# Four stretches of 64-column products in place of six, in each round of a perceiver layer's attention

## What is computed

```python
x = x + _L0_xattn_ref(_layernorm(x), ctx_1024, ctx_1024, mask, gamma, beta)   # softmax(q.k) @ v, layernorm
x = x + _L0_attn_ref(_layernorm(x), W_qkv, W_out)                             # one head of 512
x = x + _L0_ffn_ref(_layernorm(x), router_w, expert_w1, expert_w2)            # top 2 of 8 experts
```

## Time and profile before

| what | us |
|---|---|
| median of 3 runs | 757.66 (757.39 to 758.61) |
| profiled execution | 757.7 |
| span of the profiled execution | 756.0 |
| TensorE busy | 735.9 (97% of the span) |
| VectorE busy | 439.4 (58%) |
| ScalarE busy | 310.5 (41%) |
| Pool engine busy | 155.7 (21%) |

### The profile page before, as it was taken

The page is one execution under the profiler, slowest core; times in us unless marked ns, Lnnn a source line. Parts: engine busy times, 40 slices in busy tenths (PEclk is TensorE's granted clock), DMA queues, the critical chain, the costliest instruction groups (busy, mean ns, idle before and its releaser), DMA issues.

```text
span 756.0 us, 12377 instructions
## 1 busy us (share of the span) xinstructions
PE 735.9 (97%) x4786; PEld 557.9 (74%) x4786; DVE 439.4 (58%) x1003; ACT 310.5 (41%) x520; POOL 155.7 (21%) x162
## 2 busy tenths in 40 slices
PE   7999999999999999999999999999999999999996
PEld 5443454545546454478999999999999899888885
DVE  5324456676767673868865454555555665565631
ACT  2122212121212131345456455555565665656631
POOL 2132030505041301123401301310211311120201
PEclk9999999999999999999999999999999999999998
DMA  9999999999999999930635635745665756674602
GB/s 319 406 422 416 395 400 418 402 418 402 418 399 420 400 416 405 374 116 31 205 125 197 189 113 197 199 148 216 163 222 167 217 190 206 238 203 175 177 2 28
DMA packets 36477, 199.40 MB, mean 264 GB/s; under 512 B 4716, under 2 KB 5372, under 8 KB 15680
## 3 DMA queue, kind: packets, MB, share of 16 engines
q1 hardware_dynamic: 29912, 186.74, 64.3%
q0 software_dynamic: 4704, 9.14, 6.6%
q10 hardware_dynamic: 1800, 2.70, 1.1%
HBM read 188.19 MB, written 10.37 MB: 263 GB/s over the span
## 4 chain that ended last, share of the span: by engine, by line
PE 84%; DMA 7%; DVE 4%; SPq 2%; issue 1%; ACT 1%; POOL 0%; POOLq 0%
PE ps L850 11%; PE ps L809 9%; PE ps L1074 8%; PE ps L1076 8%; PE ps L1075 8%; PE ps L1096 4%; PE ps L1098 4%; PE ps L1097 4%; PE ps L1105 4%; PE ps L1106 4%; PE ps L1107 4%; PE ps L865 3%; DMA arena<-in_w_qkv 3%; DMA arena<-in_ctx 3%; PE ps L777 2%; DVE low_a L1519 2%
## 5 line engine op out<-in xcount | busy, mean ns | idle before, releaser
L481 POOL TENSOR_TENSOR small<-small 128x1 f32<-128x1 f32 x64 | 24.8, 388 | 551.2 <-DVE yb_space L1688 196.2
L1289 ACT ACTIVATE hid<-ps 128x288 f32<-128x288 f32 (+5 forms) x128 | 50.6, 396 | 145.1 <-PE ps L1076 140.9
L1076 PE MATMUL ps<-xT,low_a 128*128 128x288 f32 (+5 forms) x384 | 110.1, 287 | 0.0
L1657 DVE TENSOR_TENSOR h_ring<-hid,h_ring 128x288 fp32r<-128x288 f32 (+5 forms) x128 | 55.6, 435 | 85.2 <-ACT h_ring L1294 85.1
L850 PE MATMUL ps<-arena 128*64 128x512 f32 (+1 forms) x416 | 95.4, 599 | 1.7 <-DMA arena<-in_ctx 0.9
L1519 DVE TENSOR_TENSOR low_a<-w_raw_a,high_b 128x2048 fp32r<-128x2048 f32 x32 | 73.2, 2292 | 37.8 <-ACT high_b L1214 37.8
L809 PE MATMUL ps<-arena 128*64 128x512 f32 x384 | 85.7, 596 | 0.8 <-DMA arena<-in_ctx_turned 0.6
L1154 ACT COPY arena<-ps 128x512 f32<-128x512 f32 (+2 forms) x90 | 42.0, 526 | 100.3 <-PE ps L784 62.5
L1074 PE MATMUL ps<-xT,high_b 128*128 128x288 f32 (+5 forms) x256 | 74.9, 292 | 0.0
L1075 PE MATMUL ps<-xT,high_b 128*128 128x288 f32 (+5 forms) x256 | 73.4, 287 | 0.0
L1076 PEld LDWEIGHTS ps<-xT,low_a 128*128 128x128 f32 x384 | 72.4, 189 | 0.0
(11 more groups left out here) (217 smaller groups left out, 1639.3 us busy)
## 6 DMA issues: line engine op xcount, KB each, us to landing
arena<-in_ctx_turned SPq DMA_DIRECT2D x48, 1024.0 KB, 22.7
arena<-in_ctx SPq DMA_DIRECT2D x48, 1024.0 KB, 19.6
w_raw_a<-in_w SPq DMA_DIRECT2D x48, 1024.0 KB, 4.9
w_raw_b<-in_w SPq DMA_DIRECT2D x16, 1024.0 KB, 4.9
arena<-in_mask SPq DMA_DIRECT2D x8, 800.5 KB, 21.6
tokens_x<-arena SPq DMA_DIRECT2D x11, 256.0 KB, 13.7
arena<-in_w_qkv SPq DMA_DIRECT2D x8, 256.0 KB, 4.8
out<-res SPq DMA_DIRECT2D x8, 256.0 KB, 9.6
```

Of the source, the lines that this page charges most:

```text
L1076: mm = pe.matmul(o, w_low[2 * f][:, cols], high[:, k, 0:w.width], start=False, stop=(k == KC - 1))
L1289: nc.scalar.activation(hid[:, c % 2, 0:w.width], bank(c % UP_BANKS)[:, 0:w.width], ACT.Gelu).then_inc(gelu_done, 1)
L1657: dve.tensor_tensor(h_ring[:, c % RING, 1, 0:w.width], hid[:, c % 2, 0:w.width], h_ring[:, c % RING, 0, 0:w.width].bitcast(F32), ALU.subtr ...
```

## The change

Only orders change. Nothing is added or removed, and no operand moves to another place but for the banks.

- TensorE: all scores of a round stand together; `turn_first` and then the router follow them (before, the router stood ahead of the scores and `turn_first` between blocks 1 and 2). `ranks` and then `turn_own_probs` follow the own `values` directly (before, `ranks` stood ahead of `keys`, and `turn_own_probs` behind the first block of sums). So the first two blocks of sums are one stretch.
- VectorE: `route_first` moves from the front of the round to behind `softmax` and `low_xn`; `tops` moves ahead of `gates` and `route_second`.
- ScalarE: `gate_exp` moves behind the softmax exponential and the copy of the keys.
- `fill_order` follows with the order of the fills.

The last part behind the loop, for the last tile, keeps its order.

```diff
@@ fill_order
-        for kind, t in (("logit", r - 3), ("xn", r - 2), ("qr", r), ("rank", r - 3), ("g", r - 2), ("s", r - 2),
-                        ("u", r - 2), ("pt", r - 2), ("out", r - 2), ("xq", r + 1), ("rest0", r + 1),
+        for kind, t in (("qr", r), ("xn", r - 2), ("logit", r - 3), ("g", r - 2), ("s", r - 2),
+                        ("u", r - 2), ("rank", r - 3), ("pt", r - 2), ("out", r - 2), ("xq", r + 1), ("rest0", r + 1),
@@ TensorE
                 turn_prob(r - 1)
+                for blk in range(NBLK - 1):
+                    scores(r, blk)
+                rest_scores(r)
+                if runs(r - 2):
+                    turn_first(r - 2)
                 if runs(r - 3):
                     router(r - 3)
-                scores(r, 0)
-                scores(r, 1)
-                if runs(r - 2):
-                    turn_first(r - 2)
-                scores(r, 2)
-                rest_scores(r)
-                if runs(r - 3):
-                    ranks(r - 3)
...
                     values(r - 2)
-                sums(r - 1, PV_ORDER[1])
+                if runs(r - 3):
+                    ranks(r - 3)
                 if runs(r - 2):
                     turn_own_probs(r - 2)
+                sums(r - 1, PV_ORDER[1])
                 sums(r - 1, PV_ORDER[2])
@@ ScalarE
-                if runs(r - 3):
-                    gate_exp(r - 3)
                 exps(r)
                 if runs(r - 2):
                     copy_fill("g", r - 2, gT, shown=by_chunk)
+                if runs(r - 3):
+                    gate_exp(r - 3)
                 if runs(r - 2):
                     own_exps(r - 2)
@@ VectorE
-                if runs(r - 3):
-                    route_first(r - 3)
                 softmax(r)
                 if runs(r - 2):
                     low_xn(r - 2)
                 if runs(r - 3):
+                    route_first(r - 3)
+                if runs(r - 2):
+                    tops(r - 2)
+                if runs(r - 3):
                     gates(r - 3)
                     route_second(r - 3)
-                if runs(r - 2):
-                    tops(r - 2)
```

## The result

| what | before | after |
|---|---|---|
| median in this comparison, us | 758.61 (9 runs, 757.1 to 759.78) | 760.51 (9 runs, 759.29 to 761.95) |
| profiled execution, us | 757.7 | 760.3 |
| span, us | 756.0 | 758.6 |

The changed kernel is slower: the ratio is 1.0027, with a 95% interval of 1.0019 to 1.0036. That is some 2.0 us (1.4 to 2.7). The two profiled executions differ by 2.6. The forecast was 758.7, or +1.0 us, with a range up to 760.3. The median lies 0.2 us above that range. Of its distance of 1.8 us to 758.7, 0.95 is before's own median, which was 757.66 when the forecast was made and 758.61 here; the other 0.9 is what the change cost beyond the 1.0 forecast.

The account below looks back on a forecast made before the run. Round 3 was taken as bound by a context transfer's landing, later rounds by TensorE. The forecast was 757.7 + 2.85 (round 3) - 1.84 (four rounds at 0.46) = 758.7 us, range 756.4 to 760.3.

Parts of the forecast that it names:

- What bounds round 3: Round 3: the third block of turned context lands just before the scores that read it, margin 0.3 us.
- the DMA wait: Round 3, ahead of the third score block: TensorE waits 1.2 us for the landing at 128.84 us.
- the moved work: Round 3: 1.37 us of TensorE work moves behind the rest scores, which end only 0.26 us earlier.
- `route_first` under the mask operation: Round 3, VectorE: L621 holds L1474 to 140.28 and L1477 to 141.75 us; the round loses 2.85 us.
- the two faster rivals in which these run on: Round 3: L1477 not held, 757.7 us, chance 0.17; or no small VectorE operations held, 756.7 us, chance 0.12.
- the third: Whole gain: round 3's context block lands early enough and nothing is held, about 755.1 us; chance 0.10.
- Rounds 4 to 7: Fewer width changes on TensorE save 0.46 us a round, 1.84 us in four, with no wait for own probabilities.
- The first of the slower rivals: Rounds 4 to 6: `route_first`'s copy out of PSUM held to L621's end, 0.47 us each, 760.1 us; chance 0.10.
- The second, held to the end: Two-input VectorE operations held to L621's end; own probabilities 1.1 us late in three rounds, 762.4 us; chance 0.03.
- `weigh` and what follows keep their distance to the sums: Behind the start of the sums: the work through `weigh` keeps its earlier spacing, with no added time.
- an unseen wait on the slower side: Anywhere in the kernel: a wait the forecast did not see makes it slower, no size given; chance 0.03.

## Why the prediction was wrong

- **What bounds round 3, the DMA wait, the moved work:** right. 1.2 us forecast, 1.04 measured; E (the end of the rest scores), as the start of `turn_first` shows it, within 0.04 us, the keys to 0.01.
- **`route_first` under the mask operation:** right, L1473 held (3.85 us) and L1476, the prediction's L1477, held as taken (1.27 us). With that the two faster rivals in which these run on fall, and the wait of 1.04 us takes away the third. For L1476 there was luck in it: the forecast went by L1506, but in the same round before, another operation with one SBUF input and an SBUF result had run on under L621 in 0.15 us:

```profile
136.48 0.15 DVE L1491 TENSOR_SCALAR route<-route 128x1 f32<-128x1 f32 x1
```

  The sums began 0.39 us behind the forecast, by VectorE's pause ahead of L1399. The experiment with the late mask operation shows the mechanism: without the collision both waits are gone.
- **Rounds 4 to 7:** right in kind, 0.46 taken and 0.54 measured, so 0.3 us more in four rounds. The first of the slower rivals, a copy out of PSUM held by the mask operation, falls with round 4 of the changed kernel, where L621 runs from 173.79 to 179.42 and the copy, L1466, takes 0.15 us in it:

```profile
178.40 0.15 DVE L1466 COPY route<-ps 128x8 f32<-128x8 f32 x1
```

```profile
173.79 5.63 POOL L621 TENSOR_SCALAR arena<-arena 128x1601 f32<-128x1601 int32 x1
```

  The copy comes 4.61 us behind the start of L621. At the same distance in round 6 before, where L621 starts at 243.28, the conversion L1490, from SBUF to SBUF, was held to the end of L621:

```profile
247.89 1.05 DVE L1490 CAST route<-route 128x2 int32<-128x2 f32 x1
```

  The second, held to the end, falls with L1473, released 4.14 us into an operation of 5.62.
- **The step that failed** is "`weigh` and what follows keep their distance to the sums". It held the two joined blocks at 7.0 us; they took 8.71. The forecast had TensorE idle for two stretches of 1 us behind each other, and priced the idle time but not the clock behind it: that term stood at nothing, without a reason. The 1.69 us is missing from the sum. With it, forecast and trace agree: round 3 lost 35.25 - 30.36 = 4.89 us, of which 1.69 are the clock; the remaining 3.20 less four times 0.54 is 1.04, and the forecast was 1.0. That they agree so closely is luck: round 3 lost 0.35 us more than the 2.85 forecast, by the pause, and rounds 4 to 7 saved 0.32 more than 1.84.
- **The chances:** 0.03 stood for an unseen wait on the slower side. What was unseen was no wait, but what two known waits did to the speed of the work behind them.

Two sizes were underrated with it. The range was cut at 760.3 although the forecast's own mechanism could leave TensorE idle for 2 us, and the single median of before that it was added to moved by 0.95 us in the next comparison. On that later base 760.51 would lie inside the range, so it is the trace, more than the median, that shows the missing term. The profiled executions differ by 2.6 us and the medians by 1.9, because before's profiled execution lies 0.9 us below its median and the changed kernel's 0.2.

## What to carry to other kernels

A forecast that puts new idle time on the busiest engine should price the clock behind it too, from a stretch where it has fallen or as an open term on the slow side: here 2.04 us of waits cost 1.69 us more. When work loses the cover of a block, look for the one round in which its inputs come late; a gain of 0.54 us in four rounds is lost by one round that differs. An order that suits the steady rounds can be kept for them alone, and the collision that this moves elsewhere is then taken out by a wait on the engine that no one waits for; here the median then lay 2.35 us below before, where the whole change had cost some 2.0.

## What the runs showed of the hardware

- TensorE's granted clock fell to half for some 3.4 us behind two waits of 1.23 and 0.81 us with 0.5 us of work between them, in 3 of 3 profiles, and in 0 of 2 with the waits filled by transposes. Two waits of 0.3 and 0.8 us in the last round were followed by a fall in 4 of 12 profiles. The single wait for the context ahead of the third score block, 1.04 us here and up to 1.43 in the other kernels, was followed by none. By the Trainium skill, TensorE: Matmul & The Clock Gate, section What's actually happening, a monitor sets the clock by how busy the engine has been recently; the trace agrees, with 0.66 granted over 145 to 150 us, behind 5 us in which TensorE was busy for 3.21.
- Small VectorE operations beside a Pool operation of 5.62 us (L621) differ by their operands. In round 3 of the changed kernel L1473, with two SBUF inputs, went on 4.14 us after the start of L621, and L1476, from 128x8 to 128x8 in SBUF with one input, only at its end. The reduction L1475 (128x8 to 128x1 in SBUF) took its 0.16 us between them, and before L1491 (128x1 to 128x1 in SBUF) took 0.15. The copy L1466 with its input in PSUM was not held (0.15 us in round 4). So one input in SBUF alone does not say that an operation is held; what else it takes, no run here separates.
